# Placing the output product's matmuls between quarters of the block products in a Mamba scan

## The reference

```python
x, Bm, Cm = silu(conv(xBC))            # 64 heads x 8 values; 128 states
dA, dtx   = exp(dt * A), dt * x
state = state * dA + dtx (outer) B_t   # token by token
y_t   = C_t . state
y     = y + D * x
var   = mean(y * y)                    # over all 512 channels
out   = y * rsqrt(var + eps) * norm_w * silu(z)
return out @ out_proj_w                # 512 -> 256
```

## Time and profile before

| | us |
|---|---|
| median of 3 runs | 626.01 (625.16 to 627.05) |
| the profiled execution | 624.38 |
| its span, first to last instruction | 622.6 |
| PE busy | 524.6 (84%) |
| DVE busy | 412.3 (66%) |
| ACT busy | 264.1 (42%) |
| POOL busy | 176.2 (28%) |
| mean granted clock of TensorE | 0.933 |

### The profile page before, as it was taken

The page is one execution under the profiler, slowest core; times in us unless marked ns, Lnnn a source line. Parts: engine busy times, 40 slices in busy tenths (PEclk is TensorE's granted clock), DMA queues, the critical chain, the costliest instruction groups (busy, mean ns, idle before and its releaser), DMA issues. The chain is left out here.

```text
span 622.6 us, 18278 instructions
## 1 busy us (share of the span) xinstructions
PE 524.6 (84%) x7904; PEld 454.9 (73%) x7904; DVE 412.3 (66%) x989; ACT 264.1 (42%) x484; POOL 176.2 (28%) x185
## 2 busy tenths in 40 slices
PE   2979989999996989853797888988889838999997
PEld 1879988898985867643576677777767626989886
DVE  5998946556466999693377777886658634564633
ACT  0311324233233577882465556555446313332321
POOL 0160100000005500025565466574455420000000
PEclk9989999999999889976699999998889777999999
DMA  8400024000000000002000000000070000011011
GB/s 286 112 0 0 2 102 187 0 2 1 0 1 1 1 1 1 0 1 51 3 5 4 4 4 5 4 5 4 3 289 4 4 0 2 0 35 35 0 35 35
DMA packets 11150, 19.10 MB, mean 31 GB/s; under 512 B 3681, under 2 KB 9665, under 8 KB 10561
## 3 DMA queue, kind: packets, MB, share of 16 engines
q1 hardware_dynamic: 10416, 17.32, 7.9%
q10 hardware_dynamic: 656, 0.66, 0.4%
HBM read 10.63 MB, written 6.55 MB: 28 GB/s over the span
## 5 line engine op out<-in xcount | busy, mean ns | idle before, releaser
L243 PE MATMUL look<-diag,mask 128*128 128x256 f32 x544 | 70.4, 292 | 16.9 <-DVE mask L163 13.5
L243 PEld LDWEIGHTS look<-diag,mask 128*128 128x128 f32 x544 | 68.1, 199 | 18.9 <-issue 10.0
L300 POOL TENSOR_TENSOR n_rstd<-n_ve,m_half 128x4 f32<-128x4 f32 x12 | 12.6, 1050 | 208.9 <-DVE n_ve L296 208.9
L1031 POOL TENSOR_TENSOR w<-xdt,ends 32x512 f32<-32x512 f32 (+1 forms) x64 | 67.1, 1072 | 2.1 <-PE prior L845 1.5
L928 DVE TENSOR_TENSOR mmat<-seg,gs 128x512 f32<-128x512 f32 x64 | 42.5, 684 | 34.4 <-ACT seg L883 34.4
L587 DVE SCALAR_TENSOR_TENSOR cv<-pre,conv_w,cv 128x512 f32<-128x512 f32 x72 | 58.9, 831 | 9.1 <-ACT cv L655 8.2
L423 ACT ACTIVATE f_hT<-f_h 128x512 fp32r<-128x512 f32 (+1 forms) x48 | 30.3, 632 | 75.9 <-DVE f_h L382 75.9
L384 DVE TENSOR_TENSOR f_hT<-f_h,f_hT 128x512 fp32r<-128x512 f32 (+1 forms) x48 | 33.2, 691 | 33.5 <-ACT f_hT L423 33.5
L59 PE MATMUL f_down<-wd,f_hT 128*128 128x256 f32 x192 | 54.5, 284 | 0.0
L61 PE MATMUL f_down<-wd,f_hT 128*128 128x256 f32 x192 | 54.0, 281 | 0.0
L60 PE MATMUL f_down<-wd,f_hT 128*128 128x256 f32 x192 | 53.9, 281 | 0.0
(11 more groups left out here) (152 smaller groups left out, 1292.7 us busy)
## 6 DMA issues: line engine op xcount, KB each, us to landing
wgu_dram<-wgu SPq DMA_DIRECT2D x1, 2816.0 KB, 9.1
wgu<-wgu_dram SPq DMA_DIRECT2D x1, 2816.0 KB, 10.4
out<-x_res SPq DMA_DIRECT2D x4, 512.0 KB, 2.9
x_res<-in_x SPq DMA_DIRECT2D x1, 1536.0 KB, 14.8
wd_dram<-wd SPq DMA_DIRECT2D x1, 1536.0 KB, 12.0
wd<-wd_dram SPq DMA_DIRECT2D x1, 1536.0 KB, 13.7
win_raw<-in_in_w SPq DMA_DIRECT2D x1, 1344.0 KB, 10.8
abk<-ab SPq DMA_DIRECT2D x12, 64.0 KB, 2.0
```

The source lines that it names most:

```text
L243: ins = pe.matmul(bank[b][:, n, :, :], mask[b][:, k, P * n:P * n + P], diag[:, k, :, :], start=k == 0, stop=k == LUT - 1)
L1031: pool.tensor_tensor(heads(w[r, n, :]), heads(xdt[a % 2][r, :]), ends[a % 2][r, n * HEADS:(n + 1) * HEADS].unsqueeze(2) .broadcast_to([Q * ...
```

## The change

In the scan's PE program, the sum of squares moves from the end of the step to ahead of the block products, behind segment group 3. The 64 block products are cut into quarters of 16, and behind each quarter stand three of the twelve output matmuls. intra_ok is still raised by the last block product, out_ok by the last output matmul. Segment group 4 comes behind all of them. The other engines' programs stay as they are.

```diff
--- before.py
+++ after.py
@@ -850,28 +850,33 @@
                               ).then_inc(s["new_ok"], 1)
                 if do_a:
                     segments(a, 3)
+                if do_z:
+                    wait(pe, "yf_ok", 4 * (z + 1))
+                    wait(pe, "red_ok", z + 1)
+                    pe.matmul(yo[:, HID:HID + 1], ssum[:, 0, :], T["ones"][:, 0:1], start=True, stop=True)
                 if do_b:
                     wait(pe, "m_ok", (UNITS - 1) * (b_ + 1))
                     wait(pe, "xbd_ok", NB * (b_ + 1))
                     wait(pe, "y_ok", b_)
-                    for hh in range(HG):
-                        for g in range(4):
-                            h = HG * g + hh
-                            ins = pe.matmul(intra[Q * g:Q * g + Q, :, hh, :], mmat[b_ % 2][:, :, h], xbd[:, h, :, :],
-                                            start=True, stop=True)
-                    ins.then_inc(s["intra_ok"], 1)
+                for quarter in range(4):
+                    if do_b:
+                        for hh in range(HG // 4 * quarter, HG // 4 * (quarter + 1)):
+                            for g in range(4):
+                                h = HG * g + hh
+                                ins = pe.matmul(intra[Q * g:Q * g + Q, :, hh, :], mmat[b_ % 2][:, :, h], xbd[:, h, :, :],
+                                                start=True, stop=True)
+                        if quarter == 3:
+                            ins.then_inc(s["intra_ok"], 1)
+                    if do_z:
+                        if quarter == 0:
+                            wait(pe, "uhi_ok", z + 1)
+                            wait(pe, "ulo_ok", z + 1)
+                        ins = split_mm(pe, yo[:, 0:HID], uh[:, 0, quarter, :], uh[:, 1, quarter, :],
+                                       wout[:, 0, quarter, :], wout[:, 1, quarter, :], quarter == 0, quarter == 3)
+                        if quarter == 3:
+                            ins.then_inc(s["out_ok"], 1)
                 if do_a:
                     segments(a, 4)
-                if do_z:
-                    wait(pe, "yf_ok", 4 * (z + 1))
-                    wait(pe, "red_ok", z + 1)
-                    pe.matmul(yo[:, HID:HID + 1], ssum[:, 0, :], T["ones"][:, 0:1], start=True, stop=True)
-                    wait(pe, "uhi_ok", z + 1)
-                    wait(pe, "ulo_ok", z + 1)
-                    for k in range(4):
-                        ins = split_mm(pe, yo[:, 0:HID], uh[:, 0, k, :], uh[:, 1, k, :], wout[:, 0, k, :],
-                                       wout[:, 1, k, :], k == 0, k == 3)
-                    ins.then_inc(s["out_ok"], 1)
 
         @block.scalar
         def _(act):
```

## The result

| | before | after |
|---|---|---|
| median of the runs compared, us | 625.59 | 652.64 |
| the profiled execution, us | 624.38 | 656.85 |
| its span, us | 622.6 | 655.1 |
| mean granted clock of TensorE | 0.933 | 0.922 |

The change makes the kernel 4.6% slower: ratio 1.046, 95% interval 1.0377 to 1.0543. That is 27 us between the medians. The forecast was 655, with a range of 635 to 674. The medians are of all executions and the ratios of those that weren't slowed: one execution of a later kernel took 2663 us where its three others took 640 to 642, and why is open.

The account below looks back on a forecast made before the run. A ring of waits through all engines, with intra_ok as a link, was taken to bound the scan's step. Delay 34.7, returned stalls -14.8 and clock +9.6 gave +29.5 us on the median 626.01: 655, range 635 to 674.

Parts of the forecast that it names:

- The ring and its 11.02 us: Scan's quick step: a chain of waits through all engines, with intra_ok as a link, sets its 11.02 us.
- The term 14 x 2.4: Fourteen full scan steps: matmuls moved ahead of intra_ok delay everything behind it by 2.4 us each, 33.6 us.
- The rival (a): Order on PE: changes between small and large weights are free and the clock holds, +5, 631 us; chance 0.17.
- No gain from the earlier output product: End of the output product: ending earlier gains nothing, since ve stands behind xbd and the exponential on ACT.
- The 14.8 given back: PE's dense block products: with the stretch thinned, late instruction fetches stall less, -14.8 us of 16.25.
- the excess: Eight slower scan steps: 16.25 us over quick ones, read as PE running out of instructions in block products.
- thinning: Block products: pauses of about 0.7 us between quarters of 0.5 should let a fetch late by 1.51 us arrive.
- 1.4 beside the weight load: The step of 14.79 us beside the FFN weights' load: 1.4 us over the others' 13.36, not given back.
- The clock, +9.6: PE's rest of about 2.0 us ahead of the transposes: clock falls cost 1.2 us in eight steps, +9.6.
- The last step, +1.1: The step with only products and output: only changes of kind between matmuls count, about 1.1 us.

Follow-up runs that it names:

- Halves: The changed kernel with two groups of six output matmuls in place of four of three: ratio 1.0366, 647.39 us.
- the whole piece: The kernel before with the sum of squares and the whole output product, uncut, ahead of the block products: ratio 1.0525, 659.36 us.
- the runs with 26 and 90 matmuls: The kernel before with 26 or 90 unread small matmuls at the scan's start and 19 in each of fourteen steps: 620.74 and 650.41 us.

## Why the prediction was right

*The ring and its 11.02 us.* Right. The two runs with a second xbd break exactly the link that the prediction named, and the quick steps shrink by 1.63 and 1.03 us. The order itself stays dear, 1.9 us a step, when another link holds the ring.

*The term 14 x 2.4.* Measured 2.48 a step, 34.7 us for fourteen where 33.6 was forecast. Its parts: the sum of squares ahead took 0.42 to 0.43 (0.43 in the run that moves it alone); a group of three and its two changes of kind took 426.54 - 425.39 = 1.15 less a quarter of block products, 2.05/4 = 0.51, so 0.64 each, of which 0.28 are the changes. 0.43 + 3 x 0.64 = 2.35, the rest lies at the end of the last quarter. Halves and the whole piece fit the same prices within 0.2. The rival (a), free changes, is out. The Trainium skill (TensorE: Matmul & The Clock Gate, Part 2) says that weight loads are pulled ahead of running matmuls under two conditions; here it is no argument for (a), since 0.28 us for a pair of changes stays.

*No gain from the earlier output product.* Right: ve starts 2.65 us after its end. Moving its readers gives 0.45 us a step.

*The 14.8 given back.* That the excess is late instruction fetches was right and is shown: the runs with 26 and 90 matmuls move the stalls. That the added delay takes them away was right, too. These are PE's waits on issue in the fourteen steps of before, 14.3 us in nine places:

```profile
PE seg L804 <- issue: 5.5, 3, 2.1
...
PE intra L860 <- issue: 4.7, 4, 1.9
...
PE yo L59 <- issue: 3.0, 1, 3.0
...
PE yo L60 <- issue: 1.1, 1, 1.1
```

In the changed kernel one is left, 1.6 us in segment group 4. Two things the prediction had wrong. Only 4.7 of the 14.3 us lay within the block products, the rest behind them in segment group 4 and the output product. And thinning isn't needed: with the whole output product in one piece ahead of block products as dense as ever, 5.8 us are left. A delay ahead of the block products does most of it by itself, which is also the reason that the prediction gave for the size (the added 2.4 us is longer than the idle seen). What the pauses between the quarters add was not tested apart from it.

The size was somewhat too small. Of the 18.2 us of excess, 0.9 is left in the first step and 12.3 are in steps with a low clock, which the clock's term counts; I had left in 1.4 beside the weight load. Not all of the 18.2 was waiting on issue: the clock was low behind some of the stalls (mean 0.86 from 411 to 466 us), and the two weren't separated. The Trainium skill (Runtime: NRT & Kernel Launch, Instruction fetch mechanics) says that crossing a 16 KiB boundary is mostly hidden. By number the trace of before agrees, with waits in nine places against 40 packets of q8 in the fourteen steps. By cost it doesn't: in the kernel with 90 small matmuls these waits were 25.0 us of PE's idle time in 14 steps.

*The clock, +9.6.* Also too small. In the changed kernel seven of the fourteen steps are long at a low clock, 0.9 to 2.7 us over a quick one and 12.2 in total, so 1.7 each where the prediction took 1.2 in eight. It is 2.7 where the fall covers the whole way to segment group 3. The two sizes that were off offset each other: -14.8 + 9.6 = -5.2 was forecast, 13.2 - 18.2 = -5.0 measured. That is luck. The profiled execution of the changed kernel was also the slowest of its four (656.85 against 650.87 to 653.6), so its steps show somewhat more low clock than the median does.

*The last step, +1.1.* From the fifteenth transposes to the next it took 11.3 us against 11.73, the other way. Both ran at a low clock (0.85 and 0.74), which hides the term. The two kernels with two buffers show it at a clock of 1.00, first in the changed order, then in that of before (no xbd is written in this step): 1.5 us.

```profile
492.76:503.15 10.39, 8.36 (x205) 6.40 (x205) 5.90 (x13) 1.52 (x3) 2.14 (x3) 1.00 0.02 4
```

```profile
488.39:497.24 8.85, 7.20 (x205) 5.86 (x205) 5.82 (x13) 1.52 (x3) 2.17 (x3) 1.00 0.02 5
```

*Outside the steps.* The profiled spans differ by 32.5 us, the steps by 29.7. The first step starts 3.6 us later, at 319.90 instead of 316.35. The start moves between kernels whose programs ahead of it are the same (317.85 us with the sum of squares alone), and what moves it stays open. The medians differ by 27.

## What to carry to other kernels

Before matmuls are moved on PE, find the semaphore whose raising is a link of the step's ring, and count all that would then stand ahead of it: an engine with spare time overall can still be on the ring at one place. An earlier result is worth only as much as its first reader's queue allows, so look at what stands ahead of the reader there. Where one buffer makes the ring, a second one (here 8 KB a partition) may be worth more than an order of the matmuls; the order still has its price, so compare orders with the second buffer in place.

## What the runs showed of the hardware

- Going from small to large weights and back cost 0.28 us a pair (0.64 for three matmuls of 0.12), and this was the same in groups of three and of six within 0.03 us a step.
- PE's instructions came in packets of 16 KB, about one for 256 instructions. In the kernel with 90 small matmuls, where each step met one at the end of the block products, PE stood still there for 1.0 to 1.8 us, and for 4.5 beside the load of the FFN weights. Block products as dense, but 2.1 us later in the step, passed without a stall (the run with the output product whole). 128 more instructions ahead of the scan made the kernel 4.8% slower (620.74 to 650.41 us).
- How often the clock falls doesn't follow the length of the rest alone. With 2.26 us of rest seven steps of fourteen were long by it, with 1.9 us the mean clock was lower (0.91 against 0.92), with 1.23 it mostly held, with 0.64 it held throughout. Each is one profile.
